# Edge counts of a graph kernel: two sets of one-hot slots, matmuls in bursts, and one register load per tile of five blocks

## What is computed

```python
src = jnp.concatenate([edge_index[0], loop]); dst = jnp.concatenate([edge_index[1], loop])  # loop: nodes 0 to 624
alpha = jax.nn.leaky_relu(s[src] + d[dst])
ex = jnp.exp(alpha - m[dst])
w = ex / (segment_sum(ex, dst) + 1e-16)
out = segment_sum(h[src] * w[:, None], dst)
```

## Time and profile before

| what | value |
|---|---|
| median of 3 runs | 7331.43 us (7329.41 to 7336.07) |
| profiled execution: its own time | 7337.61 us |
| its span in the trace | 7336.1 us |
| mean granted clock of PE, share of full | 0.768 |
| count_edges in the trace | from about 866 us to the barrier at 1522.6 us |

### The profile page before, as it was taken

One profiled execution on the slowest core, in us unless ns is written; L12 is line 12 of the kernel. 1 busy time (PEld: TensorE's weight loads), 2 busy tenths in 40 slices (PEclk: granted clock), 3 DMA queues, 4 the chain that ended last, 5 costly groups with the idle time before them and its releaser, 6 DMA issues. The chain is left out here.

```text
span 7336.1 us, 100226 instructions
## 1 busy us (share of the span) xinstructions
PE 4950.6 (67%) x23535; PEld 4095.8 (56%) x23536; DVE 2728.1 (37%) x5564; ACT 2374.0 (32%) x4829; POOL 2524.9 (34%) x2090
## 2 busy tenths in 40 slices
PE   3878635535357677584989989559757766766746
PEld 2766535523245554483878868558635554555535
DVE  4444535530222212105968879400022222222143
ACT  2333124424211113343656656335311112111132
POOL 3778300022357760201000000030127773577600
PEclk7887769968766668797999989679856666576668
DMA  3333220012223320221111111022113331233300
GB/s 88 95 98 99 73 76 34 34 36 84 69 77 85 85 72 6 76 79 47 57 41 52 43 50 57 10 85 81 53 45 85 85 85 44 68 85 85 76 13 19
DMA packets 360158, 464.62 MB, mean 63 GB/s; under 512 B 191387, under 2 KB 275146, under 8 KB 360074
## 3 DMA queue, kind: packets, MB, share of 16 engines
q0 software_dynamic: 262016, 293.64, 15.8%
q1 hardware_dynamic: 79988, 152.25, 6.0%
q10 hardware_dynamic: 18070, 17.79, 0.9%
HBM read 377.19 MB, written 84.20 MB: 63 GB/s over the span
## 5 line engine op out<-in xcount | busy, mean ns | idle before, releaser
L607 POOL DMA_INDIRECT p_message<-node_table,p_index x1275 | 1554.5, 1219 | 737.0 <-ACT p_index L599 461.4
L641 PE MATMUL p_acc<-p_spread,p_message 125*128 125x160 f32 x5100 | 1357.8, 425 | 644.1 <-DVE p_spread L621 300.0
L641 PEld LDWEIGHTS p_acc<-p_spread,p_message 125*128 125x128 f32 x5100 | 1101.4, 276 | 901.1 <-issue 827.3
L2158 PE MATMUL p_acc<-p_H,p_eT 125*125 125x256 f32 x3750 | 823.5, 378 | 0.0
L1131 POOL IOTA p_order_i<- 125x200 int32 x3 | 1.1, 374 | 2359.0 <-SPq L79 2359.0
L599 ACT COPY p_index<-src_col 125x1 int32 x1275 | 240.5, 191 | 1682.4 <-PE p_acc L641 1508.4
L2158 PEld LDWEIGHTS p_acc<-p_H,p_eT 125*125 125x125 f32 x3750 | 695.0, 187 | 106.0
L886 POOL DMA_INDIRECT p_message<-edge_table,p_index x425 | 562.5, 1324 | 144.9 <-issue 128.0
L627 DVE TENSOR_TENSOR AT<-AT,p_acc 128x320 f32 x75 | 36.6, 488 | 1314.1 <-PE p_acc L641 920.1
L621 DVE TENSOR_SCALAR p_spread<-node_number,dst_value,edge_weight_col 125x160 f32 x1275 | 397.0, 385 | 198.7 <-issue 198.7
L1439 PE MATMUL p_up<-p_xT,p_w1s 128*128 128x125 f32 x3056 | 393.6, 287 | 101.9 <-ACT p_xT L1474 73.3
(11 more groups left out here) (400 smaller groups left out, 6913.7 us busy)
## 6 DMA issues: line engine op xcount, KB each, us to landing
p_count<-edge_counts SPq DMA_DIRECT2D x75, 762.9 KB
p_message<-node_table,p_index POOLq DMA_INDIRECT x1275
edge_counts<-p_total SPq DMA_DIRECT2D x25, 762.9 KB
p_rows_in<-dealt ACTq DMA_DIRECT2D x139, 125.0 KB
made<-p_rows_out SPq DMA_DIRECT2D x136, 125.0 KB
p_w1s<-in_L_ffn_W POOLq DMA_DIRECT2D x16, 1024.0 KB
p_dst_all<-dst_row SPq DMA_DIRECT2D x25, 531.2 KB
p_w2s<-in_L_ffn_Wd POOLq DMA_DIRECT2D x8, 1024.0 KB
```

The source lines that it names most:

```text
L607: pool.indirect_dma_start(message[:, k, :], None, table, bass.IndirectOffsetOnAxis(ap=index[:, k:k + 1], axis=0)).then_inc(message_ready[k ...
L641: last = pe.matmul(acc[:, h, 0:WIN], message[:, k, h * 128:(h + 1) * 128], spread[:, k], start=(k == 0), stop=(k == R_CH - 1))
L2158: last = pe.matmul(acc[:, s, 0:C], eT[:, r % 4, a % 4], H[:, a, 0:C], start=(a == 0), stop=(a == T - 1))
```

## The change

Four things change, all around `count_edges`.

1. `low` and `cell` get two full sets of four slots, by block number modulo 2, and one extra slot each for the further rounds (`low_more`, `cell_more`). `used[0..4]` become `block_used` (raised once at the end of a block, DVE may be two blocks ahead) and `more_used`.
2. PE waits once per block, for the four `cell`s and for the first further `low` and `cell` as well, and then issues its products together: slot 0, the diagonal, the further rounds, slots 1 to 3. All waits inside slots 1 to 3 are gone. The addresses of the slots now depend on the block number.
3. The two matmuls with zeros are gone in tiles 5 to 24, `none16` with them; slot 3 closes the sum. In tiles 0 to 4 the diagonal stays, at another place in the order.
4. The table has one row of six values per tile: five packed pairs and the rounds before the tile. PE and DVE load a row with one register load of six values, check each, and derive the counts before each block by adding up. `load_graph` writes the table in the new layout.

```diff
-    def block_of(self, eng, b):
-        both = eng.value_load(self.blocks[0:1, 0, tile(b)], min_val=FIRSTS, max_val=FIRSTS * FIRSTS - 1)
-        before = eng.value_load(self.blocks[0:1, 2, tile(b)], min_val=0, max_val=CH * BLOCKS)
-        return both % FIRSTS, both // FIRSTS, before
+    def blocks_of(self, nc, engine, j):
+        _, values = nc.values_load_multi_w_load_instructions(self.blocks[0:1, tile(j), :].rearrange("p j k -> p (j k)"), engines=(engine,))
+        before = nc.s_assert_within(values[TB], 0, CH * BLOCKS)
+        found = []
+        for s in range(TB):
+            both = nc.s_assert_within(values[s], FIRSTS, FIRSTS * FIRSTS - 1)
+            found.append((both % FIRSTS, both // FIRSTS, before))
+            before = before + both // FIRSTS
+        return found
...
-            then(dve.tensor_copy(own[:, 0, 0:n], q[:, 1, 0:n]))
-            prefix(n + 1, own[:, 2])
+            then(dve.tensor_copy(g.blocks[:, 0:T, 0:TB], q[:, 1, 0:n].rearrange("p (j s) -> p j s", s=TB)))
+            prefix(n, before[:])
+            then(dve.tensor_copy(g.blocks[:, 0:T, TB:TB + 1], before[:].rearrange("p (j s) -> p j s", s=TB)[:, :, 0:1]))
...
-        low = ph.sb("low", [P, LEAD + 1, P], BF16)
-        cell = ph.sb("cell", [P, LEAD + 1, BLK, T], BF16)
+        low = ph.sb("low", [P, 2, LEAD, P], BF16)
+        low_more = ph.sb("low_more", [P, P], BF16)
+        cell = ph.sb("cell", [P, 2, LEAD, BLK * T], BF16)
+        cell_more = ph.sb("cell_more", [P, BLK * T], BF16)
...
-            with dve.Fori(0, BLOCKS) as b:
-                first, rounds, before = g.block_of(dve, b)
-                dve.wait_ge(used[LEAD - 1], b + 1)
-                dve.tensor_tensor(low[:, 0:LEAD], ...
-                for k in range(LEAD):
-                    cells(b, k, first + k)
-                with dve.Fori(0, rounds) as i:
-                    dve.wait_ge(used[LEAD], before + i + 1)
-                    dve.tensor_scalar(low[:, LEAD], ...
-                    cells(b, LEAD, first + i + LEAD)
+            with dve.Fori(0, T) as j:
+                for s, (first, rounds, before) in enumerate(g.blocks_of(nc, DVE, j)):
+                    b = j * TB + s
+                    mine = turn_of(nc, b)
+                    dve.wait_ge(block_used, b + 1)
+                    dve.tensor_tensor(low[:, mine], ...
+                    for k in range(LEAD):
+                        cells(cell[:, mine, k].rearrange("p a n -> p (a n)"), b, first + k)
+                    with dve.Fori(0, rounds) as i:
+                        dve.wait_ge(more_used, before + i + 1)
+                        dve.tensor_scalar(low_more[:], ...
+                        cells(cell_more[:], b, first + i + LEAD)
...
-            def products(j, s, loops):
+            def products(j, s, own_blocks, loops):
                 b = j * TB + s
-                _, rounds, before = g.block_of(pe, b)
+                _, rounds, before = own_blocks[s]
+                mine = turn_of(nc, b)
+                left = low[:, mine].rearrange("p a k n -> p (a k) n")
+                right = cell[:, mine].rearrange("p a k n -> p (a k) n")
+                v = before + b * LEAD
                 pe.wait_ge(block_kept, b + 1)
-                pe.wait_ge(low_ready, before + b + 1)
-                for k in range(LEAD):
-                    add(at, before + b * LEAD + k, k, start=(k == 0))
+                pe.wait_ge(low_ready, before + b + 2)
+                pe.wait_ge(ready, v + LEAD + 1)
+                add(at, left[:, 0], right[:, 0], start=True)
+                if loops:
...
                 with pe.Fori(0, rounds) as i:
                     pe.wait_ge(low_ready, before + b + i + 2)
-                    add(at, before + b * LEAD + i + LEAD, LEAD)
...
-                last.then_inc(block_done, 1)
+                    pe.wait_ge(ready, v + i + (LEAD + 1))
+                    add(at, low_more[:], cell_more[:]).then_inc(more_used, 1)
+                for k in range(1, LEAD):
+                    last = add(at, left[:, k], right[:, k], stop=(k == LEAD - 1))
+                last.then_inc(block_used, 1)
...
             def step(j, loops):
-                products(j + 1, 0, loops)
+                own_blocks = g.blocks_of(nc, PE, j + 1)
+                products(j + 1, 0, own_blocks, loops)
                 turns(j)
```

More of the change, by code:

```diff
@@ L28 @@
 PE, DVE, ACTIVATION = mybir.EngineType.PE, mybir.EngineType.DVE, mybir.EngineType.Activation
+PE, DVE, ACTIVATION = mybir.EngineType.PE, mybir.EngineType.DVE, mybir.EngineType.Activation
 N, E, C = 3125, 53125, 256
@@ L212, in load_graph @@
         qi = ph.sb("qi", [1, 128], I32)
+        before = ph.sb("before", [1, BLOCKS], I32)
         round_ends = ph.sb("round_ends", [1, 2, ROUNDS])
@@ L337, in tile_of @@
                 then(dve.tensor_scalar(out, qi[:, 0:n], 19, None, ALU.arith_shift_right))
-            first, count, before = (g.tiles[0:1, :, k] for k in range(3))
+            first, count, visits = (g.tiles[0:1, :, k] for k in range(3))
             then(dve.memset(g.tiles[:], 0))
             tile_of(q[:, 0, 0:n], first[:, 0:n])
-            tile_of(round_ends[:, 0], before[:, 0:n])
-            then(dve.tensor_tensor(qi[:, 0:n], before[:, 0:n], first[:, 0:n], ALU.subtract))
+            tile_of(round_ends[:, 0], visits[:, 0:n])
+            then(dve.tensor_tensor(qi[:, 0:n], visits[:, 0:n], first[:, 0:n], ALU.subtract))
             then(dve.tensor_scalar(count[:, 0:n], qi[:, 0:n], 1, None, ALU.add))
             then(dve.tensor_copy(q[:, 2, 0:n], count[:, 0:n]))
-            prefix(n, before)
+            prefix(n, visits)
             dve.wait_ge(counted, 4)
@@ L672, in count_edges @@
         low_ready = ph.sem("low_ready")
-        used = [ph.sem(f"used{k}") for k in range(LEAD + 1)]
-        block_done = ph.sem("block_done")
+        block_used = ph.sem("block_used")
+        more_used = ph.sem("more_used")
         block_kept = ph.sem("block_kept")
@@ L700, in _ @@
             then(dve.tensor_copy(base[:], base_i[:]))
-            for k in range(LEAD + 1):
-                dve.sem_inc(used[k], 1)
+            dve.sem_inc(block_used, 2)
+            dve.sem_inc(more_used, 1)
             dve.sem_inc(block_kept, 2)
             dve.sem_inc(flip_kept, 4)
-            def cells(b, k, c):
-                dve.tensor_scalar(cell[:, k].rearrange("p d h -> p (d h)"), g.iota[:, 0:BLK * T], base[:, tile(b)], key[:, chunk_at(nc, c)],
-                                  ALU.add, ALU.is_equal).then_inc(ready, 1)
@@ L710, in _, with cells @@
-            with dve.Fori(0, BLOCKS) as b:
-                first, rounds, before = g.block_of(dve, b)
-                dve.wait_ge(used[LEAD - 1], b + 1)
-                dve.tensor_tensor(low[:, 0:LEAD], g.iota[:, 0:P].unsqueeze(1).to_broadcast([P, LEAD, P]),
-                                  lo[:, chunk_at(nc, first, LEAD)].unsqueeze(2).to_broadcast([P, LEAD, P]), ALU.is_equal).then_inc(low_ready, 1)
-                for k in range(LEAD):
-                    cells(b, k, first + k)
-                with dve.Fori(0, rounds) as i:
-                    dve.wait_ge(used[LEAD], before + i + 1)
-                    dve.tensor_scalar(low[:, LEAD], g.iota[:, 0:P], lo[:, chunk_at(nc, first + i + LEAD)], None, ALU.is_equal).then_inc(low_ready, 1)
-                    cells(b, LEAD, first + i + LEAD)
+            def cells(out, b, c):
+                dve.tensor_scalar(out, g.iota[:, 0:BLK * T], base[:, tile(b)], key[:, chunk_at(nc, c)], ALU.add, ALU.is_equal).then_inc(ready, 1)
@@ L724, in _, with add @@
             pe.wait_ge(setup, SETUP)
-            def add(at, v, k, start=False):
-                pe.wait_ge(ready, v + 1)
+            def add(at, left, right, start=False, stop=False):
                 for h, (d, n) in enumerate(HALVES):
-                    last = pe.matmul(at[:, h, 0:n * T], low[:, k], cell[:, k, d:d + n].rearrange("p d h -> p (d h)"), start=start, stop=False)
-                last.then_inc(used[k], 1)
-            def products(j, s, loops):
+                    last = pe.matmul(at[:, h, 0:n * T], left, right[:, d * T:(d + n) * T], start=start, stop=stop)
+                return last
@@ L756, in step @@
             def step(j, loops):
[L757 removed]
+                own_blocks = g.blocks_of(nc, PE, j + 1)
+                products(j + 1, 0, own_blocks, loops)
                 turns(j)
                 for s in range(1, TB):
[L760 removed]
+                    products(j + 1, s, own_blocks, loops)
+            own_blocks = g.blocks_of(nc, PE, 0)
             for s in range(TB):
[L763 removed]
+                products(0, s, own_blocks, True)
             with pe.Fori(0, LOOPED - 1) as j:
```

22 lines of the change are left out of this document (11 added, 11 removed).

## The result

The change made the kernel a little faster: 7300.50 us, the median of 5 runs (7295.03 to 7303.41), against 7332.81 us before. The ratio is 0.9956, with a 95% interval from 0.9943 to 0.9969. That is 32 us gained where 66 were forecast. The range (7207 to 7310) holds the time, but the size of the gain was forecast at twice its value.

A forecast was written before the change was run, and what follows sets the result against it. No engine is full; a chain through PE's sequencer and its register loads bounds the tile. Blocks 13.0, load 3.2 and transposes 3.3 make 19.5 us against 22.28, gaining 66 us: 7265 us, range 7207 to 7310.

The forecast's parts named there:

- The place of the gain: In count_edges, nothing gained before 1001 us; then one load of 3.2 us a tile in place of five gaps.
- the granted clock stays near 0.9: PE in count_edges: mean clock of 0.91 kept, adding 0.2 us to each block.
- the 2.8 that the prediction named as a sign of being wrong: PE's burst of a block: the prediction is wrong if it takes over 2.8 us from first product to last.
- a rival: PE's clock falls to 1.2 GHz for the rest of the tile after the load's pause: tile 25.5, 7400 us; chance 0.07.
- this trace doesn't bear it out at 3 us: Argument against clock loss on PE: gaps of 3.10 us within the tile were followed by products of 1.56, at full clock.
- The load group: Once a tile on PE: six-value load 1.2 us, six checks 1.8, adding up and loop head 0.2, together 3.2.
- The blocks: PE and its sequencer: 2.4 us plus 0.2 for the clock, 2.6 a block, 13.0 for five.
- All three are covered by PE: DVE (15 us a tile), ACT (9.9) and the store of total (6.6) fit inside PE's 19.5 us tile.
- From the tile to the time: 22 intervals x (22.28 - 19.5) = 61 us, last interval 4.7, together 66 us off 7331.4.

The follow-up runs named there:

- The packed load alone: The kernel before with only the table and its load changed, one register load of six values per tile on PE and DVE; 7295.75 us, ratio 0.9951.
- The filler run: The changed kernel with four added fp32 matmuls, result overwritten, that PE runs while its sequencer loads and checks the table row; 7259.70 us, ratio 0.9900.
- static sets: The changed kernel with three sets of slots at fixed addresses, blocks of a tile using 0, 1, 0, 1, 2; 7269.65 us, ratio 0.9913.
- the rows of eight: The changed kernel with table rows of eight values, the same six loaded, each row starting at a multiple of 32 bytes; 7286.54 us, ratio 0.9938.
- filler and rows of eight: The changed kernel with three fixed-address sets of slots, four added matmuls in PE's load gap and table rows of eight values; 7210.81 us, ratio 0.9837.
- sets and bursts alone: The changed kernel with two register loads per block as before, two sets of slots and bursts kept; 7391.03 us, ratio 1.0081.

## Why the prediction was right in direction and wrong in size

*The place of the gain* was right. The five gaps for register loads became one, the first store's landing held everything up to about 1002 us, and the phase gained from there on. The packed load alone shows that this step carries the whole gain.

*The sum, cut where the trace can be cut.* The terms of the forecast put the head of a block, the sequencer's work ahead of its first product, with the block; the trace shows block 0's head inside the pause. Cut alike, in us a tile:

| stretch | forecast | measured |
|---|---|---|
| block 0, from its first product to the transposes | 2.6 - 0.5 = 2.1 | 2.66 |
| transposes | 3.7 | 3.92 |
| blocks 1 to 4 | 4 x 2.6 - 0.4 = 10.0 | 10.05 |
| pause ahead of block 0 | 3.2 + 0.5 = 3.7 | 3.81 |
| tile | 19.5 | 20.44 |

0.8 of the missing 0.9 us lie in block 0 and the transposes behind it.

*The clock*: this is the step that failed. I kept the mean clock of before, 0.91, for all blocks and the transposes ("the granted clock stays near 0.9"), which gave block 0 the same 0.2 us for the clock as any other. Measured is 0.80, and block 0 comes 0.9 us dearer in every tile. Its 2.87 us also reach the 2.8 that the prediction named as a sign of being wrong. The transposes are busy for 75.73 / 19 = 3.99 us a tile, where 2.99 is their time at full clock:

```profile
1066.00:1454.40 388.40, 75.73 (x475) 76.82 (x475) 0.80 0.10 38
```

With the clock at 0.98 the tile is 18.75 us, so the clock's price is 1.7 us a tile. That is no more than the forecast had set aside in all (0.2 for each of five blocks, and 3.7 against 2.99 for the transposes); it set it aside at the wrong place, and needed 0.8 of it for something else, as the blocks show.

The prediction named this cause as a rival, with a price of 6 us a tile and a chance of 0.07, and set against it that pauses of 3.10 us had been followed by bursts at full clock. That reading held for the one tile it looked at. In the same trace of before, in nine of the 19 tiles, a pause of 3.15 to 3.31 us is followed by a burst of 2.86 or 2.87 us. One of them lies one tile earlier, with a granted clock of 0.50 from 1433.3 to 1436.3 us:

```profile
1433.37 2.87 PE L729 MATMUL p_acc<-p_cell,p_low 125*125 125x325 bf16 x10 [3.19 <-DVE p_cell L707]
```

The transposes of before take 2.99 us in one tile and 4.4 to 4.6 in the next, but for one of 3.33, and 3.7 is the mean. So the sentence "this trace doesn't bear it out at 3 us" was wrong, and the rival had more for it than 0.07, though at a smaller price: the effect doesn't last all tile. The length of the pause alone doesn't decide it either, since 3.48 us with the load alone left block 0 at 1.95, and block 3 above is slow behind 0.48. The Trainium skill ("TensorE: Matmul & The Clock Gate", HAM oscillation) describes waits for transfers that drop the clock ahead of every group of matmuls; here the pause is sequencer work, and the trace after agrees, with 2.87 us for block 0 in all 19 tiles. The filler run confirms it: PE works in the pause, and block 0 and the transposes run at full clock.

*The load group* was sized well: I took 3.2 us, measured are 0.82 and 1.47 us for the load, 1.15 in the mean against 1.2, and checks at 0.3. From the last check to block 0's first product PE's sequencer needs another 0.7 us (1384.9 to 1385.60).

*The blocks*: the sum for blocks 1 to 4 was right, 10.05 us against 10.0, but by luck. The pace is set by DVE (2.8 us a block), whose register work grew as well, and not by PE's sequencer and the clock (2.4 + 0.2): at a granted clock of 0.98 they take as long. My 2.53 us for DVE left that work out; with static sets DVE starts a block 2.55 us after the one before.

*"All three are covered by PE"* was wrong. I compared 15 us of DVE work a tile with 19.5 of PE's and called DVE covered. The two are coupled through few slots: DVE stands while PE transposes (2.33 us at 1393.24), and after its own load it is ready for block 0 only some 0.1 us before PE. A second load on DVE cost 0.8 us a tile, where the prediction would give zero.

*From the tile to the time*: 22 intervals x (22.28 - 20.44) = 40.5 us, and the last interval 14.7 instead of 18.9 gives 4.2, together 44.7 by this sum and 43.1 in the trace, where I had 61 + 4.7. The runs' medians show 32. The other 10 us lie in the choice of the profiled executions: that of before was 4.8 us above the median of its five runs (7337.61 against 7332.81), that of the changed kernel 5.5 us below.

What stays open: what decides whether a burst behind a pause is slow; why the transposes took longer after the shorter pause (4.12 and 4.38 us behind 3.50, 3.90 behind 4.15), which ate the gain of the rows of eight; and why DVE's load of a row took longer with static sets (medians of 1.24 us with them alone and 1.18 with filler and rows of eight, against 0.82 with the filler alone). What the kernel would gain without the six range checks after the load (6 x 0.3 = 1.8 us a tile) was not tried.

## What to carry to other kernels

A pause that is gathered from many short ones into one long one can cost PE its clock, and then the work behind the pause pays: before grouping register work, look which bursts follow the longest gaps and at what length they run, and look at several tiles: here every second tile of the trace before showed the slow burst, and the one that was read did not. Split a change into its parts and run each alone; here one half brought the whole gain and the other half was a loss of 60 us by itself. When two engines hand a few slots to each other, compare their times between two hand-overs and not over the whole tile.

## What the runs showed of the hardware that I had not expected

- A register load of six values takes 0.82 us or 1.47 us on PE (0.82 or 1.41 on DVE), by where the row starts in the table: rows 24 bytes apart alternate, rows 32 bytes apart are all fast (on DVE not with static sets, 1.18 us). A single value takes 0.30.
- After 3.5 to 4.15 us of idle PE ran ten matmuls in 2.87 us, in every tile of the changed kernel; kept busy by fillers it ran them in 1.97, and the transposes behind them in 2.99 instead of about 4.0. With the packed load alone the burst was slow only behind 4.13 us, and before the change in nine of 19 tiles behind 3.15 to 3.31.
- PE's bursts with all addresses but those of the extra slot from registers take 1.95 us for ten matmuls at full clock, and 2.41 with two more such addresses. Where only the PSUM address comes from a register they take 1.78 with the loop of rounds in the middle of the burst and 1.56 with the loop at its end, as before the change.
- With bursts 0.9 us apart the clock can still stay low: in the run with sets and bursts alone it was 0.64 in the mean.
